# First batch of expert routing inside the recurrence: where the choosing, the ranks and the places stand in VectorE's order

## The reference, cut to what matters

```python
logits = x @ router_w                      # (2048, 16)
assign = jnp.argmax(logits, axis=-1)
w = jax.nn.sigmoid(jnp.take_along_axis(logits, assign[:, None], axis=1)[:, 0])
hh = gelu(jnp.einsum('nd,edf->nef', x, w1) + b1)
all_out = jnp.einsum('nef,efd->ned', hh, w2) + b2
out = jnp.take_along_axis(all_out, assign[:, None, None], axis=1)[:, 0, :] * w[:, None]
```

## Time and profile before

| what | value |
|---|---|
| time before, median of 3 runs (lowest, highest) | 685.11 us (685.09, 685.81) |
| the profiled execution's own time | 684.28 us |
| its span in the profile | 682.2 us |
| around the span | 2.1 us |
| mean granted clock of PE | 0.983 of full speed |
| PE busy, PE weight loads busy | 641.0 us (94%), 547.5 us (80%) |
| DVE, ACT, POOL busy | 421.7, 302.7, 254.8 us |
| the recurrence's steps 1 to 7 | from about 45 us to about 175 us of the span |

### The profile page before, as it was taken

The page is one execution under the profiler, slowest core; times in us unless marked ns, Lnnn a source line. Parts: engine busy times, 40 slices in busy tenths (PEclk is TensorE's granted clock), DMA queues, the critical chain, the costliest instruction groups (busy, mean ns, idle before and its releaser), DMA issues.

```text
span 682.2 us, 26441 instructions
## 1 busy us (share of the span) xinstructions
PE 641.0 (94%) x10978; PEld 547.5 (80%) x10978; DVE 421.7 (62%) x1384; ACT 302.7 (44%) x1017; POOL 254.8 (37%) x387
## 2 busy tenths in 40 slices
PE   5899999999759989999999999999999999999995
PEld 4567777777649977888888888888887999989995
DVE  3777777777633326577777686868676554444442
ACT  1456666643025414545545554545454353333331
POOL 1455666556710031131525252524243432322325
PEclk9899999999969999999999999999999999999999
DMA  7899200000048210000000000000221667566462
GB/s 191 287 299 308 57 3 2 4 6 19 25 137 244 82 43 7 7 9 7 20 12 20 14 18 16 16 16 12 97 77 26 225 223 240 186 214 225 154 241 62
DMA packets 50486, 65.69 MB, mean 96 GB/s; under 512 B 5168, under 2 KB 40208, under 8 KB 47424
## 3 DMA queue, kind: packets, MB, share of 16 engines
q1 hardware_dynamic: 44992, 57.22, 26.8%
q0 software_dynamic: 2912, 6.03, 2.6%
q10 hardware_dynamic: 2464, 0.76, 0.5%
HBM read 49.45 MB, written 18.87 MB: 100 GB/s over the span
## 4 chain that ended last, share of the span: by engine, by line
PE 59%; DVE 2%; DMA 1%; ACT 1%; issue 0%; SPq 0%; DVEq 0%
PE bank L1924 7%; PE quad L1782 6%; PE quad L1906 6%; PE quad L1908 5%; PE bank L1807 4%; PE pair L1744 3%; PE bank L1830 3%; PE quad L1788 2%; PE pair L1746 2%; PE pair L1745 2%; PE bank L1840 2%; PE pair L1769 2%; PE bank L1843 2%; PE bank L1833 2%; PE bank L1926 1%; PE quad L1911 1%
## 5 line engine op out<-in xcount | busy, mean ns | idle before, releaser
L2183 DVE TENSOR_TENSOR h_masked<-quad,const 128x1536 f32<-128x1536 f32 (+2 forms) x66 | 112.6, 1706 | 59.9 <-PE quad L1788 54.1
L2021 ACT ACTIVATE f_sa<-quad 128x256 f32<-128x256 f32 (+1 forms) x115 | 40.3, 352 | 91.6 <-PE quad L1908 75.8
L2202 DVE TENSOR_TENSOR f_hid<-f_sa,quad 128x256 f32<-128x256 f32 (+1 forms) x115 | 43.1, 380 | 53.6 <-ACT f_sa L2021 53.5
L2403 POOL DMA_INDIRECT moe_slots<-g_pay,g_slot x28 | 28.9, 1034 | 77.2 <-PE bank L1852 68.7
L1924 PE MATMUL bank<-wall,f_hid 128*128 128x128 f32 x390 | 50.7, 277 | 1.1 <-DVE f_hid L2205 0.9
L1924 PEld LDWEIGHTS bank<-wall,f_hid 128*128 128x128 f32 x390 | 47.8, 192 | 3.6 <-DVE f_hid L2205 2.8
L1906 PE MATMUL quad<-f_xT,wall 128*128 128x256 f32 (+1 forms) x190 | 50.0, 345 | 0.5 <-DVE f_hid L2202 0.5
L1908 PE MATMUL quad<-f_xT,wall 128*128 128x256 f32 (+1 forms) x190 | 49.2, 341 | 0.0
L1998 ACT ACTIVATE h_gT<-bank 128x128 f32<-128x128 f32 x64 | 17.8, 278 | 66.2 <-PE bank L1833 66.2
L1782 PE MATMUL quad<-h_qk 32*128 32x128 f32 x1024 | 46.5, 296 | 0.3 <-DVE h_masked L2183 0.3
L1782 PEld LDWEIGHTS quad<-h_qk 32*128 32x128 f32 x1024 | 34.3, 185 | 9.5 <-issue 7.0
(11 more groups left out here) (414 smaller groups left out, 1791.2 us busy)
## 6 DMA issues: line engine op xcount, KB each, us to landing
wall<-moe_w SPq DMA_DIRECT2D x23, 1088.0 KB, 5.1
moe_slots<-blank SPq DMA_DIRECT2D x2, 2112.0 KB, 24.4
wall<-in_experts_dram SPq DMA_DIRECT2D x1, 4120.0 KB, 21.8
e_w<-in_experts_dram SPq DMA_DIRECT2D x15, 257.5 KB, 3.3
moe_slots<-blank SPq DMA_DIRECT2D x1, 1984.0 KB, 9.7
moe_slots<-e_yg SPq DMA_DIRECT2D x7, 256.0 KB, 3.7
f_xg<-moe_slots SPq DMA_DIRECT2D x12, 132.0 KB, 4.1
moe_w<-in_moe_w_dram SPq DMA_DIRECT2D x1, 1408.0 KB, 7.2
```

The costliest lines, as they stand in the source:

```text
L2021: act.activation(sa[g % 3][:, 0:s], up_bank(n, f)[:, 0:s], ACT.Silu).then_inc(f_sa, 1)
L2183: dve.tensor_tensor(masked[k % 4][:, :, a * P:z * P], quad[:, :, a * P:z * P], cst("causal")[:, None, a * P:z * P].to_broadcast([P, HPG, ( ...
L2202: dve.tensor_tensor(hid[n % 2][:, f, 0:s], sa[g % 3][:, 0:s], up_bank(n, f)[:, T1:T1 + s], ALU.mult)\
L2403: pool.indirect_dma_start(out=t["moe1_slots"], out_offset=bass.IndirectOffsetOnAxis(ap=slot[:, b * 2 + k:b * 2 + k + 1], axis=0), in_=pay[ ...
```

## The change

Six edits, all for batch 0 of the routing:

1. `chosen(0, range(8))` leaves step 5; two columns each are chosen in steps 3, 4, 5 and 6, behind m = 0 and ahead of `normalise`.
2. `one_hot(0)` moves from step 5 to step 6, behind the last of these.
3. In step 6, at m = 5, DVE copies the ranks (128x144) from `bank[3]` to a new tile `ranked0` in SBUF, and PE waits for this copy ahead of `mix(7)` in place of `place_of`'s eighth instruction.
4. `place_of(0)` reads `ranked0` and moves from m = 4 to behind the copies into `att`, ahead of `moe_input(5)`.
5. PE's `keep_on(3)` in step 5, ahead of its wait for `att`, is taken out.
6. A semaphore and a tile are added for this.

```diff
@@ rwkv_phase @@
-        s_slab, s_next = sem("s_slab"), sem("s_next")
+        s_slab, s_next, s_rankc = sem("s_slab"), sem("s_next"), sem("s_rankc")
+        ranked0 = sb("r_ranked0", [P, WIDEST, E0])
@@ place_of (DVE) @@
-                ranked = bank[3 if k == 0 else 1][:, 0:(count + 1) * E0].rearrange("p (c e) -> p c e", e=E0)
+                ranked = (ranked0[:, :, :] if k == 0 else
+                          bank[1][:, 0:(count + 1) * E0].rearrange("p (c e) -> p c e", e=E0))
                 here = slice(0, count + 1)
-                dve.wait_ge(s_rank, k + 1)
+                if k == 0:
+                    dve.wait_ge(s_rankc, 1)
+                else:
+                    dve.wait_ge(s_rank, k + 1)
@@ step (DVE) @@
                     if i == CHUNKS - 1 and m == 0:
                         chosen(1, range(8, 10))
+                    if 3 <= i < CHUNKS - 1 and m == 0:
+                        chosen(0, range((i - 3) * BATCH, (i - 2) * BATCH))
+                    if i == CHUNKS - 2 and m == 0:
+                        one_hot(0)
                     if tail and m == 0:
                         normalise(i - 1, 1 - q)
@@
                     if m == 4:
-                        if i == CHUNKS - 2:
-                            place_of(0)
                         if tail:
                             dve.wait_ge(s_zg, i)
                         gate(i)
                         if tail:
                             output(i - 1, 1 - q)
+                    if i == CHUNKS - 2 and m == 5:
+                        dve.wait_ge(s_rank, 1)
+                        dve.tensor_copy(ranked0[:, :, :], bank[3][:, 0:WIDEST * E0].rearrange("p (c e) -> p c e", e=E0))\
+                            .then_inc(s_rankc, 1)
                 if prepare:
                     mix(i + 1)
                 if i == 0:
                     input_statistics(*REST)
-                if i == CHUNKS - 3:
-                    chosen(0, range(8))
-                    one_hot(0)
@@
                     dve.tensor_copy(att[rows, :, rows], leafs[rows, :, :]).then_inc(s_att, 1)
+                if i == CHUNKS - 2:
+                    place_of(0)
                 if i == CHUNKS - 1:
                     place_of(1)
                 if tail:
@@ step (PE) @@
                 if i == CHUNKS - 2:
-                    pe.wait_ge(s_place, 8)
+                    pe.wait_ge(s_rankc, 1)
                 if prepare:
                     mix(i + 1)
@@
-                if i == CHUNKS - 3:
-                    keep_on(3)
                 pe.wait_ge(s_att, i * 4 + 4)
```

## The result

| | before | changed |
|---|---|---|
| median of 22 runs (lowest, highest) | 686.87 us (684.68, 694.02) | 690.64 us (687.98, 695.11) |
| ratio, 95% interval | | 1.0062 (1.0047 to 1.0077) |
| span of the profiled execution | 682.2 us | 690.9 us |

The change makes the kernel slower by 0.62%, 4.3 us of 687 (3.2 to 5.3). Two things about the base. The three runs known beforehand were at the low end of what this kernel does: over 22 runs its median is 686.87, not 685.11. And single executions differ by several us. So the two spans (8.7 us apart) can't be compared as wholes; the ratio can.

The account below looks back on a forecast made before the run. The prediction took DVE's steps, chained by the state update, to bound the kernel. Its terms -2.3 (step 5), +2.5 (step 6) and +1.1 (clock) gave +1.3 and a forecast of 686.4 us, range 684.6 to 688.3.

Parts of the forecast that it names:

- the clock: Start of step 7: PE idles 3.0 us, its clock falls and filler records run slow; +1.1 us, bounds 0 and +2.4.
- step 6: Update to update in step 6: moved `place_of` delays POOL's `nrstd` and so the state update; +2.5 us.
- step 5: Choosing all eight columns leaves DVE's path in step 5, with nothing taking its place; -2.30 us.
- The choosing hidden in steps 3 to 6: Two columns a step, cost 0.5 us, fit in DVE's 1.23 us wait for POOL's deviation; no added time.
- the +0.25: Step 6, `one_hot`: its cast may wait for POOL's power to end, delaying `normalise`; +0.25 us, bounds 0 and 0.5.
- Gate and mix, -0.64: Step 6: without `place_of` at m = 4, DVE's mix comes sooner by PE's idle time ahead of it; -0.64 us.
- place_of behind att, 2.37: Step 6: `place_of` takes 2.37 us on DVE between `att` and `moe_input`, with no wait covering it.
- Cast to nrstd, taken as 2.9 with 3.63 as the bound: POOL, step 6: two sends keep `nrstd` behind the cast; 2.9 us, without a pause blamed on DVE's copies; bounds 2.9 and 3.63.
- the first send is long for itself: Rival, step 6: POOL's first send is slow for being first, so 3.63 us again; +2.0, 687.2 us; chance 0.12.
- "same" at 0.46: Chance of 0.46 that the whole kernel's time can't be told from no change, some 0.2% or 1.4 us.
- The rival in which `place_of` is covered: Step 6: `nrstd` comes independently of the sends, so DVE's wait covers `place_of`; sum -1.8, 683.3 us; chance 0.08.

Follow-up runs that it names:

- r7: The changed kernel with PE's `keep_on(3)` fillers put back into step 5; 1.0071 times the kernel before.
- r10: The changed kernel with POOL's wait for the blank slots moved from ahead of step 6's first send to the end of step 4; 1.0051 times before.
- r11: The kernel before with the choosing moved, step 5's fillers out, step 6's second send behind `moe_deviation`, and POOL's slot wait moved to step 4; 0.9948 times before.
- r6: The kernel before with the choosing moved, step 5's fillers out and step 6's second send behind `moe_deviation`, `place_of` left at m = 4; 0.9963 times before.
- r4: The changed kernel with POOL's second send of step 6 moved behind `moe_deviation`; 1.0056 times the kernel before.
- r1: The changed kernel with eight more filler products on PE in its pause ahead of step 7; 1.0022 times the kernel before.
- r12: The changed kernel with step 6's second send behind `moe_deviation` and five more filler products on PE ahead of step 7; 1.0021 times before.
- r5: The kernel before, unchanged, profiled and timed again; 0.9986 times the kernel before.
- r9: The changed kernel with one unused indirect gather issued by POOL at the end of step 4; 1.0071 times the kernel before.
- r3: The changed kernel with the choosing and fillers put back into step 5, so only the rank copy and `place_of` are moved; 1.0084 times before.

## Why the prediction was wrong

The range ended at 688.3 us, 1.0047 times the median it started from; the kernel is at 1.0062, 690.64 us. Of the 4.2 us between the forecast of 686.4 and the measured median, 1.8 are the base, which three runs had put too low; the rest is the sum. The mechanisms are those of the forecast, each of them seen and then separated. Three terms of the sum were off, all the same way: the clock by 1.7 us, step 6 by 0.55, step 5 by 0.3.

- *Step 5, -2.3.* It is -2.0 in every profile with the choosing moved and the fillers out (-1.2 in r7, where they are in). DVE's timeline of the changed kernel has a 0.20 us pause for "issue" between two aggregates of `moe_input` in this step, not in step 4, nor in step 5 of before. The row was right and the place it fell in wasn't free to the last tenth.
- *The choosing hidden in steps 3 to 6.* Right: steps 3 and 4 are 17.35 and 17.17, in the second profile of before 17.36 and 17.17, and `normalise` starts when POOL is done. The cast took 0.17 beside POOL's power (139.13 to 139.30, within 138.75 to 139.78), not until its end, so the +0.25 was nothing. (The exclusive lock that the Trainium skill has in "SBUF — State Buffer", "SBUF: two separate sides", doesn't show on it here; the 0.55 of the earlier trace rows does go with it. The page limits the lock to some kinds of DVE instruction, which the prediction left out, and no row here shows which kind the cast was.)
- *Gate and mix, -0.64.* Right: -0.71, and then DVE waits for PE's mix (1.26).
- *place_of behind att, 2.37.* Right: 155.95 - 153.57 = 2.38, with no cover.
- *Cast to nrstd, taken as 2.9 with 3.63 as the bound.* **This failed.** It is 3.75 here, 3.63 in the rival "the first send is long for itself", to which I gave 0.12. The rival had the right size and a wrong reason. I took the 0.88 us pause for a block by DVE's copies because they ended at that instant in one trace. They aren't there in the changed kernel and the pause is; r10 shows that it is a passed wait for a DMA's semaphore. (By the box on fp32 copies in the same section of the Trainium skill it should have gone, and r11's send would have been held up by the copies; the measurement decides.) This is 0.85 more than the 2.9 of the sum. The missing cast delay and the mix gave back 0.3 by luck, so step 6 is +3.05, not +2.5.
- *The clock, +1.1 with bounds 0 and +2.4.* It fell, as forecast, but **the size failed**: 2.0 in the first profile, 2.8 in the mean of seven. I priced eight filler records and stopped, from a slow stretch of 4.8 busy us in the earlier trace rows. That row was itself only the busy end of a longer one. The slow stretches here are 6.9 or 10.4 us, so the six records behind, the leaf scores and the `output` product run in them too. The bound of +2.4 counted the six records and nothing else, and the four profiles with 10.4 us are above it. This is the largest part of the miss.
- The sum by the rows of the changed kernel is -2.0 + 3.05 + 2.8 = +3.9 us (2.8 is the mean of seven profiles), and the measured one 4.3 (3.2 to 5.3): within what the runs can tell, nothing of the loss is left to explain.

Of the chances, "same" at 0.46 was too high because the forecast sat on the edge of what can be told and its two unsure terms (the send's pause and the length of the slow stretch) could, by their rows, mostly go up. The rival in which `place_of` is covered would have needed POOL's `nrstd` ahead of the sends; r6 and r11 make half of that true and gain from it.

## What to carry to other kernels

Before moving work into an engine's idle stretch, ask what ends the stretch: DVE's 2.14 us wait for `nrstd` was not cover for `place_of` but the tail of a POOL queue that `place_of` itself feeds, so the work pushed the end of the wait ahead of it. A queue's order is worth reading for things that stand ahead of a critical instruction without being needed by it; moving one DMA issue behind it gained 1.2 us of step 6, and with `place_of` at its old place as well. And where a change opens a pause of PE of some us, put fillers into it, or count the time behind it at the lower clock until the trace shows it back up, not only up to the first dependency.

## What the runs showed of the hardware

- A passed wait is not free on POOL ahead of an indirect DMA: 0.88 us from the cast to the send with it, 0.31 without (r10, r11), and 0.29 in a later batch, whose code has no such wait.
- The clock fell in all seven profiles with a pause of PE of 2.6 to 3.9 us ahead of step 7, and stayed at the lower level for 6.9 us in three and 10.4 in four, though PE was busy nearly all through once it went on (9.9 of 9.9 us in r4). Pauses of 0.44 and 0.48 there did nothing (r1, r12). In between the length alone doesn't tell: the clock fell behind 1.09, 1.28, 1.55 and 1.82 us, and not behind 1.27, 1.49 and 1.56 (steps 1 and 2; 1.49 is in the tail of before).
- In both kernels single executions lose time in a step ahead of the change: step 2 is 17.3 to 17.8 us with no pause of PE or one of under 0.5, 18.6 and 18.8 with a pause of 1.3 and 1.6 (r5, r9), and 20.1 to 22.9 where the clock fell behind it as well (changed, r1, r3, r4). The rest behind the gate product differs by 3.8 us between profiles too, without a cause shown. Together these are a good part of the 9 us over which the runs of before spread, though its step 6 repeats to 0.01 us, and they are why a ratio here needs a dozen runs and more.
